# Local attention in a two-layer perceiver kernel: weights in three whole key blocks with constant zeros, and the values of four heads weighed in one run

## The reference, cut to what matters

```python
for i in range(DEPTH):
    x = attn_layer(shift_tokens(x), Wqkv[i], q_scale[i], k_scale[i], Wo[i]) + x
    x = ffn_layer(shift_tokens(x), ln_g[i], ln_b[i], W1[i], b1[i], W2[i], b2[i]) + x
```

## Time and profile before

| | us |
|---|---|
| median of three runs | 5058.57 (5054.35 to 5061.95) |
| the profiled execution's own time | 5055.65 |
| its span | 5053.7 |
| TensorE busy (matmul) in the span | 4552.4, 90% |
| VectorE, ScalarE, GpSimd busy | 3254.5, 2900.7, 1877.3 |
| granted TensorE clock, mean | 0.97 |

### The profile page before, as it was taken

The page is one execution under the profiler, slowest core; times in us unless marked ns, Lnnn a source line. Parts: engine busy times, 40 slices in busy tenths (PEclk is TensorE's granted clock), DMA queues, the critical chain, the costliest instruction groups (busy, mean ns, idle before and its releaser), DMA issues. The chain is left out here.

```text
span 5053.7 us, 86339 instructions
## 1 busy us (share of the span) xinstructions
PE 4552.4 (90%) x32008; PEld 3054.5 (60%) x32008; DVE 3254.5 (64%) x7543; ACT 2900.7 (57%) x5798; POOL 1877.3 (37%) x1876
## 2 busy tenths in 40 slices
PE   5889998989699999999999999948999999759999
PEld 3555555547456666666666666635555555448888
DVE  5677777767565655656565565536777777575555
ACT  3666666668455656566565665615666666523332
POOL 3222232125454544445454444313222222025554
PEclk8999999999899999999999999979999999879999
DMA  6655555400200010100101000046556555111110
GB/s 136 128 102 106 106 113 107 77 23 1 70 23 15 24 33 12 53 13 14 44 12 53 5 23 24 4 98 136 111 102 113 107 106 89 24 49 48 47 48 22
DMA packets 189934, 305.64 MB, mean 60 GB/s; under 512 B 19736, under 2 KB 109752, under 8 KB 187832
## 3 DMA queue, kind: packets, MB, share of 16 engines
q1 hardware_dynamic: 189520, 300.13, 27.1%
HBM read 215.81 MB, written 73.40 MB: 57 GB/s over the span
## 5 line engine op out<-in xcount | busy, mean ns | idle before, releaser
L707 DVE TENSOR_REDUCE xa_m_part<-xa_ring 128x1 f32<-128x512 f32 x2048 | 1319.4, 686 | 505.8 <-PE xa_ring L856 491.5
L633 ACT ACTIVATE xa_ex<-xa_sc 128x1024 f32<-128x1024 f32 x1024 | 991.6, 1022 | 109.8 <-PE xa_sc L844 95.0
L856 PE MATMUL xa_ring<-xa_ks,xa_q_base 48*128 48x512 f32 x2048 | 517.8, 497 | 183.2 <-DVE xa_m_part L707 129.7
L870 PE MATMUL xa_pv<-xa_ex,xa_vs 128*17 128x256 f32 x8192 | 549.4, 386 | 4.2 <-issue 4.2
L856 PEld LDWEIGHTS xa_ring<-xa_ks,xa_q_base 48*128 48x128 f32 x2048 | 200.9, 185 | 515.3 <-DVE xa_m_part L707 433.6
L1572 POOL TENSOR_TENSOR lt_r_qk<-lt_r_qk,lt_t_rot 128x512 f32<-128x512 f32 x192 | 243.5, 1269 | 695.1 <-DVE lt_t_rot L1688 691.2
L1038 ACT ACTIVATE lt_p<-lt_bank,lt_stat,lt_rq 128x128 f32<-128x128 f32 (+1 forms) x768 | 366.2, 482 | 216.4 <-DVE lt_stat L1009 211.2
L844 PE MATMUL xa_sc<-xa_q_base,xa_ks 50*128 50x256 f32 x4096 | 423.1, 302 | 26.8 <-ACT xa_k L605 5.8
L844 PEld LDWEIGHTS xa_sc<-xa_q_base,xa_ks 50*128 50x128 f32 x4096 | 347.1, 187 | 117.4 <-ACT xa_vs L620 24.4
L1026 POOL TENSOR_SCALAR lt_p<-lt_p,lt_stat 128x192 f32<-128x192 f32 x384 | 339.9, 889 | 203.4 <-DVE lt_stat L1016 203.4
L2414 PE MATMUL moe_bank<-moe_xp,moe_wp 128*128 128x512 f32 x1536 | 373.3, 392 | 5.9 <-POOL moe_wp L2242 4.2
(11 more groups left out here) (283 smaller groups left out, 8962.8 us busy)
## 6 DMA issues: line engine op xcount, KB each, us to landing
xa_ks<-keys SPq DMA_DIRECT2D x384, 256.0 KB, 9.3
keys<-xa_kp SPq DMA_DIRECT2D x128, 512.0 KB, 3.8
xa_cx<-in_ctx_t SPq DMA_DIRECT2D x64, 512.0 KB, 4.6
lt_wqk<-in_lt_wqkv SPq DMA_DIRECT2D x6, 2048.0 KB, 9.0
lt_w<-in_lt_w SPq DMA_DIRECT2D x6, 1536.0 KB, 7.1
xa_q_base<-xa_m_rows SPq DMA_DIRECT2D x512, 2.0 KB
moe_w<-in_moe_wg SPq DMA_DIRECT2D x64, 128.0 KB, 2.1
moe_w<-in_moe_wu SPq DMA_DIRECT2D x64, 128.0 KB, 2.3
```

What stands on the lines that cost most here:

```text
L633: act.activation(x.ex[:, n % x.NE, :, :], x.sc[n % 2][:, :, :], ACT.Exp).then_inc(*x.ex_done.one())
L707: dve.tensor_reduce(x.m_part[:, i % 2, qt, h, ch:ch + 1], x.bank(n + odd), AX.X, ALU.max).then_inc(*x.dve_out.one())
L856: pe.matmul(x.bank(n + odd), x.q_base[rows, pair, b * S + qt * P:b * S + (qt + 1) * P], x.ks[unit % x.NU][rows, pair % 4, ch * 512:(ch + 1 ...
L870: mm = pe.matmul(x.pv[32 * j:32 * j + x.VW, :], x.vs[:, i % x.NV, kt, 4 * g + j, :], x.ex[:, n % x.NE, 2 * (j % 2) + j // 2, :], start=(kt ...
```

## The change

`p` gets three whole blocks of 128 columns: tile 0's weights in columns 0 to 127, tile 1's in 192 to 383 (`place`), and zeros in 128 to 191 of all five buffers, written once by VectorE (after the mask's copy, since the mask is loaded through `p`). The turn becomes three transposes of 128 by 128; the banks' memsets go. With `side` = 2 a call covers four heads: the first two write columns 0 to 255 of the output bank, the other two 256 to 511, and one eviction moves 512 columns. The ring `pt` grows from four to six heads. `rot` goes: SyncE loads its contents into `tab` for every layer, behind a wait for the rotations of the layer before last, and VectorE multiplies in place. `Conv` keeps `side` = 1 and its instructions. Counts that other steps wait for follow (pv_done and o_out per four heads, small_in 2, wq_in 4).

```diff
@@ Attention.__init__
-    def __init__(self, c, name, ctx, banks, n_pt, at_once, rounds, skip):
+    def __init__(self, c, name, ctx, banks, n_pt, at_once, rounds, skip, side=1):
+        self.call = at_once * side
+        self.place = (0, P + skip)
-        self.blocks = ((slice(0, P), slice(0, P), slice(0, P)),
-                       (slice(P, 2 * P - skip), slice(skip, P), slice(P, 2 * P)),
-                       (slice(2 * P - skip, self.width), slice(0, P), slice(2 * P, 3 * P)))
@@ steps
-                if len(full) == self.at_once + 1:
+                if len(full) == self.call + 1:
@@ pe_step, turn
-            for cols, rows, to in self.blocks:
-                out, src = self.t_banks[n % 2][rows, to], self.p[:, n % 5, cols]
-                if rows.start:
-                    tr = pe.matmul(out, src, self.c.ident[:, :], start=True, stop=True)
-                else:
-                    tr = pe.transpose(out, src, self.c.ident[:, :])
+            for i in range(3):
+                at = slice(i * P, (i + 1) * P)
+                tr = pe.transpose(self.t_banks[n % 2][:, at], self.p[:, n % 5, at], self.c.ident[:, :])
@@ pe_step, apply
-            for first, cols, keys, kt in ((True, slice(0, 2 * P), slice(0, 2 * P), 0),
-                                          (False, slice(P, 2 * P), slice(2 * P, 3 * P), 1)):
-                for j, head in enumerate(heads):
...
+            for side in range(self.side):
+                at = side * 2 * P
+                for first, cols, keys, kt in ((True, slice(at, at + 2 * P), slice(0, 2 * P), 0),
+                                              (False, slice(at + P, at + 2 * P), slice(2 * P, 3 * P), 1)):
+                    for j in range(self.at_once):
+                        m = self.at_once * side + j
...
@@ pool_step
-            sv = self.p[:, n % 5, P:self.width]
+            sv = self.p[:, n % 5, self.place[1]:3 * P]
@@ act_step, turn
-                on.wait_ge(self.pv_done, (n - self.n_pt) // self.at_once + 1)
+                on.wait_ge(self.pv_done, (n - self.n_pt) // self.call + 1)
@@ Local.__init__
-            self.at = Attention(c, "lt", ctx, (self.banks[0:2], self.banks[2:4], self.banks[4]), 4, 2, 1, WINDOW)
+            self.at = Attention(c, "lt", ctx, (self.banks[0:2], self.banks[2:4], self.banks[4]), 6, 2, 1, WINDOW, 2)
@@ Local.keep
-        act.activation(self.ot[:, heads[0] // 2, :], bank[:, 0:S], ACT.Copy).then_inc(*self.at.o_out.one())
+        hp = heads[0] // 2
+        act.activation(self.ot[:, hp:hp + 2, :], bank[:, :].rearrange("p (h s) -> p h s", h=2),
+                       ACT.Copy).then_inc(*self.at.o_out.one())
@@ Local.sp
-        sp.dma_start(self.rot[:, :, :, :],
-                     g("lt_rot").rearrange("p (a b c) -> p a b c", a=4, b=2)).then_inc(*self.small_in.one())
@@ Local.sp, load_front
+                on.wait_ge(self.rot_done, 3 * 8 * B * (l - 1))
+                sp.dma_start(self.tab[:, i, :, :, :],
+                             g("lt_rot").rearrange("p (a b c) -> p a b c", a=4, b=2)).then_inc(*self.wq_in[i].one())
@@ Local.dve, load_mask
-                for i in (2, 3):
-                    dve.memset(self.banks[i][:, :], 0.0).then_inc(*self.bank_zero.one())
+                on.wait_ge(self.mask_ready, 1)
+                dve.memset(self.at.p[:, :, P:P + WINDOW], 0.0).then_inc(*self.p_zero.one())
@@ Local.dve, tables
-                on.wait_ge(self.rot_done, 3 * 8 * B * (l - 1))
...
-                    dve.tensor_tensor(self.tab[:, i, :, tile, :], self.rot[:, :, tile, :], self.scl[:, i, :, :],
-                                      ALU.mult).then_inc(*self.tab_done.one())
+                    tab = self.tab[:, i, :, tile, :]
+                    dve.tensor_tensor(tab, tab, self.scl[:, i, :, :], ALU.mult).then_inc(*self.tab_done.one())
```

More of the change, by code:

```diff
@@ L919 @@
     LAG = 3
-    def __init__(self, c, name, ctx, banks, n_pt, at_once, rounds, skip):
+    def __init__(self, c, name, ctx, banks, n_pt, at_once, rounds, skip, side=1):
         nc = c.nc
-        self.c, self.at_once, self.rounds = c, at_once, rounds
+        self.c, self.at_once, self.rounds, self.side = c, at_once, rounds, side
+        self.call = at_once * side
         self.s_banks, self.t_banks, self.o_bank = banks
         self.keys, self.first, self.off = (P, 2 * P - skip), (0, skip), (0, P)
+        self.place = (0, P + skip)
         self.width, self.n_pt, self.step = sum(self.keys), n_pt, P // at_once
-        self.blocks = ((slice(0, P), slice(0, P), slice(0, P)),
-                       (slice(P, 2 * P - skip), slice(skip, P), slice(P, 2 * P)),
-                       (slice(2 * P - skip, self.width), slice(0, P), slice(2 * P, 3 * P)))
         self.p = ctx.enter_context(nc.sbuf_tensor(f"{name}_p", [P, 5, 3 * P], F32))
@@ L973, in pe_step @@
             on.wait_ge(self.t_out, n - 1)
-            for cols, rows, to in self.blocks:
-                out, src = self.t_banks[n % 2][rows, to], self.p[:, n % 5, cols]
-                if rows.start:
-                    tr = pe.matmul(out, src, self.c.ident[:, :], start=True, stop=True)
-                else:
-                    tr = pe.transpose(out, src, self.c.ident[:, :])
+            for i in range(3):
+                at = slice(i * P, (i + 1) * P)
+                tr = pe.transpose(self.t_banks[n % 2][:, at], self.p[:, n % 5, at], self.c.ident[:, :])
             tr.then_inc(*self.t_full.one())
         elif kind == "apply":
-            heads, call = h, n // self.at_once
+            heads, call = h, n // self.call
             round_ = call % self.rounds
@@ L986, in pe_step @@
                 on.wait_ge(self.o_out, call // self.rounds)
-            for first, cols, keys, kt in ((True, slice(0, 2 * P), slice(0, 2 * P), 0),
-                                          (False, slice(P, 2 * P), slice(2 * P, 3 * P), 1)):
-                for j, head in enumerate(heads):
-                    mm = pe.matmul(self.o_bank[self.step * j:self.step * j + self.step, cols],
-                                   st.v_of(b, kt, head), self.pt[:, (n + j) % self.n_pt, keys],
-                                   start=first and round_ == 0,
-                                   stop=not first and round_ == self.rounds - 1)
+            for side in range(self.side):
[4 more added lines that the diff above has]
+                        m = self.at_once * side + j
+                        mm = pe.matmul(self.o_bank[self.step * j:self.step * j + self.step, cols],
+                                       st.v_of(b, kt, heads[m]), self.pt[:, (n + m) % self.n_pt, keys],
+                                       start=first and round_ == 0,
+                                       stop=not first and round_ == self.rounds - 1)
             mm.then_inc(*self.pv_done.one())
@@ L1037, in act_step @@
                 at = slice(self.off[q], self.off[q] + self.keys[q])
-                act.activation(self.p[:, n % 5, at], s[:, at], ACT.Exp, bias=t3[:, 1, q:q + 1],
+                to = slice(self.place[q], self.place[q] + self.keys[q])
+                act.activation(self.p[:, n % 5, to], s[:, at], ACT.Exp, bias=t3[:, 1, q:q + 1],
                                scale=st.scale_of(b, h, slice(q, q + 1)) if st.scale is None else st.scale,
@@ L1047, in act_step @@
         elif kind == "apply":
-            call = n // self.at_once
+            call = n // self.call
             if call % self.rounds == self.rounds - 1:
@@ L1748, in dve @@
                 on.wait_ge(self.gen_full, self.use[step] + 1)
-                on.wait_ge(self.small_in, 3)
+                on.wait_ge(self.small_in, 2)
                 if j:
@@ L1787, in pe @@
         on.wait_ge(self.mask_ready, 1)
-        on.wait_ge(self.bank_zero, 2)
+        on.wait_ge(self.p_zero, 1)
         for step in self.plan:
```

15 lines of the change are left out of this document (7 added, 8 removed).

## The result

| | before | after |
|---|---|---|
| median, us | 5060.26 (5054.35 to 5069.72, 4 runs) | 4988.99 (4982.85 to 4998.52, 4 runs) |
| profiled execution / its span, us | 5055.65 / 5053.7 | 4998.52 / 4996.6 |
| local stage in the profiled execution, start of its first to start of its last instruction, us | 1336.9 to 3333.6: 1996.7 | 1337.5 to 3262.4: 1924.9 |
| period of a job in the stage, us | 79.99 | 76.13 in some jobs, 77.8 in the others |

The ratio is 0.9859 with a 95% interval of 0.9837 to 0.9881: 1.4% faster, 71 us. I had forecast 4946 us with a range of 4895 to 4990, so the sign is right, and the time lies at the very upper end of the range: 112 us were forecast, and 40 of them did not come. Two of the four runs, 4990.96 and 4998.52, lie above the range.

What follows compares the result with a forecast made beforehand. TensorE, 97% busy, bounds the local stage. Gross 7.5 us per job less 2.9 us lost to waits leaves 4.65, 112 us over 24 jobs: 4946 us median, own range 4920 to 4970, eight in ten 4895 to 4990.

Steps and rivals of the forecast that it cites:

- Turns: In the local stage, three transposes per head take 0.33 us instead of 0.73: 6.4 us per job, 154 us gross.
- Merging: Values of four heads in one call: each merged pair saves 0.28 us, 1.12 us per job, 27 us gross.
- Heads 0 to 2 and 6: Waits on GpSimd's divisions: 0.80 us per job lost before head 2's turn, 1.26 us before head 6's.
- The last head: At the job's end, the turn ends sooner but ScalarE is still copying values: 0.3 us per job lost.
- The gate: Feed-forward transpose waits for a bank VectorE frees behind ScalarE's gate: room 1.24 us, 0.5 us per job lost.
- The clock: TensorE's granted clock stays at 1.00 in the local stage, as it does through the present wait before head 2's turn.
- the signs: Expected in the trace: turns of 0.33 us, period some 75.3 us, waits before heads 2 and 6, clock 1.00 in the stage.
- Rival 3: Waits before heads 2 and 6 each bring 6 us at half clock: 32 us slower, 5091 us; chance 0.04.
- The other parts: Table loads per layer, memsets at the stage's start and larger evictions cost nothing; late table loads at most 45 us.
- rival 2: Heads 7 to 10 also arrive at waits, leaving 3.15 us per job: 76 us, 4983 us; chance 0.20.

Runs made afterwards that it cites:

- run with one table: Gate with the exponential in place of the gelu, so no table loads: on the changed kernel 4945.08 us (0.9774), on the kernel before 5052.56 us (0.9996).
- the kernel with the last four heads joined: Against the kernel with the transposes alone, calls of heads 12-13 and 14-15 stand together at the job's end, evictions after both: 4946.87 us.

## Why the prediction was right, and where it was not

**Turns.** 0.73 us to 0.33: as forecast. With 384 turns the gross gain on TensorE's queue is 154 us. The Trainium skill's figure of 81 ns ("TensorE: Matmul & The Clock Gate", section "Back-to-back issue gap") would have given 0.24; the traced 0.11 decided rightly.

**Merging.** Its price was right (0.28 forecast, 0.30 measured alone, 1.45 us a call against 1.47), its worth was not. I added it to the turns as though each took off its own time. On top of the transposes it has the opposite sign, since it moves calls out of time that was free, at head 6's division and above all at the gate. My prediction holds a sentence on such a move, a call "that moves two heads later", only as a loss at the gate, and I did not ask where it goes.

**Heads 0 to 2 and 6.** That GpSimd is the releaser and that these savings become waits was right: of TensorE's time in heads 0 to 6 only 0.41 us is saved, out of three turns' 1.20. GpSimd's timeline of the kernel after has the divisions of heads 2 and 6:

```profile
2175.97 0.76 POOL L1028 TENSOR_SCALAR lt_p<-lt_p,lt_stat 128x192 f32<-128x192 f32 x1
...
2185.99 1.83 POOL L1028 TENSOR_SCALAR lt_p<-lt_p,lt_stat 128x192 f32<-128x192 f32 x1
```

They end at 2176.73 and 2187.82, and the turns start 0.11 and 0.10 us later. The waits are 1.94 us in two pieces against 2.3, and 0.93 against about 1.3. Heads 0 to 6 lose the 0.8 us that were forecast, and heads 6 to 10 lose 1.09 (four turns and one merging are 1.88, and 0.79 arrived) against 1.26.

**The last head.** 0.3 us were forecast as lost; the wait for the copy grew from 0.58 to 0.74, by 0.16. By the fronts this part loses 0.11: four turns' 1.60 less the 0.39 of the calls are 1.21, and 1.10 arrived.

**The gate.** This is the step of the sum that failed: "room 1.24 us ... 0.5 us is lost". TensorE's timelines have the first feed-forward products that feed the gate, after and before:

```profile
2192.89 3.62 PE L1875 MATMUL lt_bank<-lt_ft,lt_w 128*128 128x256 f32 x16
...
2307.07 3.62 PE L1871 MATMUL lt_bank<-lt_ft,lt_w 128*128 128x256 f32 x16
```

From there to the transpose behind the gate's last product (2213.41 after, 2327.45 before) it is 20.52 us after, and was 20.38 before. Out of heads 10 to 15 the change takes five turns' 2.00 us, and three calls of 0.95 us for one of 1.62, another 1.23. Of these 3.23 us 1.58 arrived; 1.65 were lost, not 0.5. Against these 1.15 us stand losses smaller by 0.17 at head 6 and by 0.19 at the last head, and 0.79 us per job, 19 us, is what the period missed. The step itself was the start of the chain: the forecast let every saving ahead of head 13's scores through, and the chain, which runs from gate to gate, let none through. The run with one table confirms it: 1.70 us per job come back on the kernel after, none on the one before.

**The clock.** "Inside the stage it keeps 1.00 through the present wait" was right, and the conclusion for a wait of some 2 us was not. That the clock would keep 1.00 in the stage was also among the signs, and its fall inside the stage was named as one of being wrong; on this point the forecast was wrong. Rival 3 had the mechanism, a chance of 0.04 and a size of 6 us for each wait; what came was its small form, 3.4 us at half clock, behind the first of the two waits in 12 of 24 jobs and once more in the last job, 22 us in all. I had let it decide only over a change of sign and not taken a smaller case of it into my own sum or range.

**The other parts.** The tables, the memsets and the larger evictions showed no wait, as assumed: the periods of jobs in which a layer begins differ by less than 0.3 us from the others, and the eviction took what was set down for it (the groups of lines of the kernel after):

```profile
L1480 ACT ACTIVATE lt_ot<-lt_bank 128x512 f32<-128x512 f32 x96 | 57.3, 597 | 41.4 <-PE lt_bank L992 41.4
```

96 of 597 ns, where 0.60 us was taken.

**Right by the range.** 4989 lies inside 4895 to 4990 because that range reached for rival 2, which gives back 1.5 us more per job. The time is near rival 2's (4983), the places are others: gate and clock, not heads 7 to 10. My own sum missed by 43 us, and the range of 4920 to 4970 that went with it did not hold; that a loss of another kind brought the time just inside the wider range, by 1 us, is luck. (The losses of 2 to 4 us per job that it names would have given 4926 to 4975.)

## What to carry to other kernels

When work is taken off the bounding engine, follow each saving to the next wait and ask on what that wait's chain starts: a chain that begins at its own predecessor (gate to gate here) keeps its length whatever the bounding engine saves, takes in every saving, and may hold costs, like two table loads, that were free until now. Work that stands in another engine's shadow costs nothing there; moving or merging it is a loss if it lands where the engine is the bound, so merge only work that stands where the engine is the bound already, and best where it fills a wait. And a wait that grows by half a microsecond (here from 1.46 us to 0.29 and 1.65) can drop TensorE's clock behind it, in which case useless products in the gap can be cheaper than the gap.

## What the runs showed of the hardware that I had not expected

TensorE's granted clock fell to half for 3.4 us behind waits of 0.29 and 1.65 us, in 12 of 24 jobs that are otherwise equal to some 0.02 us, and never behind the 1.46 us of before; with 1.82 us of products in that gap it never fell. The same two waits brought seven such stretches with the transposes alone and two in the kernel with the last four heads joined. The jobs that it hits mostly come in a regular order; what sets that order was not settled. ScalarE's change of table costs 1.28 us each way, without anything beside it (the next instruction starts 1.30 us after the load does), and nothing at all as long as the engine that waits for it is later still. And an instruction of VectorE on two columns takes 0.87 us instead of 0.16 while GpSimd adds two tiles of 512 columns, so what is moved on GpSimd also changes the time of VectorE's small steps.
